# The last batch of an attention and expert kernel in another order: second group's scores in halves beside the first group's exponentials, batch 6's routing later

## The reference, cut to what matters

```
q = layernorm(x); k = v = ctx                 # (8, 256, 512)
qh, kh, vh = each.reshape(8 * 8, 32, 512)     # 8 heads of 32 rows
sm = softmax(einsum('bdm,bdn->bmn', qh, kh) / sqrt(32))
x = x + tanh(g) * einsum('bmn,bcn->bcm', sm, vh).reshape(8, 256, 512)
...
n = layernorm(x).reshape(2048, 512)
shared = (silu(n @ w_up_g) * (n @ w_up_y)) @ w_down
top 6 of sigmoid(n @ w_gate); position = running count per expert, over all tokens in order
routed = sum over 6 experts of weight * (silu(g) * v) @ w_down[e]
x = x + tanh(g) * (shared + routed)
```

## Time and profile before

| | |
|---|---|
| median of 3 runs | 1052.45 us (1051.8 to 1053.76) |
| the profiled execution's own time | 1051.3 us |
| its span, first to last instruction | 1049.5 us |
| TensorE busy | 990.5 us, 94% of the span |
| VectorE, ScalarE, POOL busy | 603.0, 335.0, 465.1 us |
| mean granted TensorE clock | 0.992 of full |
| main loop's last stages, batch 7's attention to the last scatter | some 637 to 720 us of the span |

### The profile page before, as it was taken

The page is one execution under the profiler, slowest core; times in us unless marked ns, Lnnn a source line. Parts: engine busy times, 40 slices in busy tenths (PEclk is TensorE's granted clock), DMA queues, the critical chain, the costliest instruction groups (busy, mean ns, idle before and its releaser), DMA issues.

```text
span 1049.5 us, 15353 instructions
## 1 busy us (share of the span) xinstructions
PE 990.5 (94%) x5629; PEld 603.6 (58%) x5630; DVE 603.0 (57%) x1249; ACT 335.0 (32%) x491; POOL 465.1 (44%) x457
## 2 busy tenths in 40 slices
PE   7999989999999999999999998895999999999886
PEld 6986545564564564464465452344777777776432
DVE  3334554765765855746756747543655556553566
ACT  3411024124133233323333231442444434443221
POOL 2000025526557467477467544352355555556000
PEclk9999999999999999999999999898999999999999
DMA  8793279697680590680610409356899999965998
GB/s 321 284 385 127 103 256 332 222 357 293 232 327 28 209 336 1 234 311 1 238 68 32 152 32 363 153 206 265 303 373 387 371 370 368 371 255 208 380 417 322
DMA packets 93622, 262.23 MB, mean 250 GB/s; under 512 B 10454, under 2 KB 10582, under 8 KB 92784
## 3 DMA queue, kind: packets, MB, share of 16 engines
q1 hardware_dynamic: 43760, 146.18, 38.0%
q10 hardware_dynamic: 31872, 63.97, 16.3%
q0 software_dynamic: 17920, 51.15, 12.4%
HBM read 129.91 MB, written 139.72 MB: 257 GB/s over the span
## 4 chain that ended last, share of the span: by engine, by line
PE 68%; DVE 8%; POOL 7%; DMA 7%; issue 6%; ACT 2%; SPq 0%; POOLq 0%; ACTq 0%; DVEq 0%
PE banks L1273 17%; PE banks L1892 11%; PE banks L1283 10%; DMA e_eo<-y_d 6%; PE banks L1881 6%; PE banks L1901 6%; POOL t_psum L773 5%; PE banks L1391 5%; PE banks L1453 5%; DVE t_nmx L1064 2%; PE banks L1471 2%; ACT t_probs L864 2%; DVE t_nmx L1073 1%; PE banks L1265 1%; PE banks L1456 1%
## 5 line engine op out<-in xcount | busy, mean ns | idle before, releaser
L1715 POOL DMA_INDIRECT y_d<-e_eo,e_ids x128 | 124.5, 973 | 126.3 <-DVE e_eo L1812 93.6
L1064 DVE TENSOR_REDUCE t_nmx<-banks 128x4 f32<-128x2048 f32 x56 | 128.1, 2287 | 58.3 <-PE banks L1391 58.3
L773 POOL TENSOR_TENSOR t_psum<-t_psum,t_probs 128x512 f32<-128x512 f32 x104 | 128.7, 1268 | 61.9 <-ACT t_probs L864 61.0
L864 ACT ACTIVATE t_probs<-banks 128x2048 f32<-128x2048 f32 x56 | 105.2, 1878 | 139.7 <-PE banks L1456 115.8
L785 POOL DMA_INDIRECT xs_d<-r_norm,r_xaddr x96 | 95.9, 998 | 49.2 <-issue 24.9
L1453 PE MATMUL banks<-b_qry,b_key 32*128 32x512 f32 x512 | 73.9, 647 | 7.9 <-ACT t_probs L864 5.7
L743 POOL TENSOR_TENSOR f_rstd<-f_veps,mhalf 128x2 f32<-128x2 f32 x24 | 16.8, 699 | 144.2 <-DVE f_veps L962 144.2
L1881 PEld LDWEIGHTS banks<-ident,e_xg 128*128 128x128 f32 x512 | 56.9, 143 | 34.3 <-issue 34.1
L1881 PE MATMUL banks<-ident,e_xg 128*128 128x128 f32 x512 | 63.9, 280 | 12.5 <-DMA e_xg<-xs_d 12.5
L773 POOL TENSOR_TENSOR t_psum<-t_probs,t_probs 128x512 f32<-128x512 f32 x52 | 66.5, 1316 | 12.4 <-ACT t_probs L864 6.3
L1391 PE MATMUL banks<-b_key,b_qry 32*128 32x512 f32 x448 | 63.9, 639 | 3.7 <-DVE t_nmx L1064 2.0
(11 more groups left out here) (227 smaller groups left out, 1646.7 us busy)
## 6 DMA issues: line engine op xcount, KB each, us to landing
xs_d<-zero ACTq DMA_DIRECT2D x32, 1056.0 KB, 7.1
e_xg<-xs_d SPq DMA_DIRECT2D x32, 1056.0 KB
y_d<-zero ACTq DMA_DIRECT2D x24, 1024.0 KB, 7.5
e_xg<-y_d SPq DMA_DIRECT2D x16, 768.0 KB, 14.8
e_eo<-y_d SPq DMA_DIRECT2D x16, 768.0 KB, 14.4
wo<-in_wud SPq DMA_DIRECT2D x6, 768.0 KB, 11.9
wupT<-in_wud SPq DMA_DIRECT2D x6, 768.0 KB, 11.7
a_x<-in_x SPq DMA_DIRECT2D x8, 512.0 KB, 4.7
```

The costliest lines, as they stand in the source:

```text
L773: ins = g_.tensor_tensor(psum0[:, q, :], first[:, q, :], probs[s % NP][:, q, :], ALU.add)
L864: A(probs[s % NP][:, :, :], quad[:, :, :], ACT.Exp, scale=SCALE1).then_inc(W["exp_ok"], 1)
L1064: V.tensor_reduce(nmx[g][:, m, :], quad[:, :, :], axis=AX.X, op=ALU.max, negate=True).then_inc(W["mx_ok"], 1)
L1715: g_.indirect_dma_start(out=y_d, out_offset=bass.IndirectOffsetOnAxis(ap=ids[:, HC * p + n:HC * p + n + 1], axis=0), in_=eo[u][:, n, :], i ...
```

## The change

It changes the tail of `ENDING` and what depends on it.

- The pieces of batch 7: before S0, S1 (halved), S2, S3 (halved), S4, S5, S6 (halved), S7, all ahead of the first Q. After: S0, S1 (halved), S2, S3 for the first group; then its P and M; and all four tiles of the second group halved, eight pieces in the pair, one after each Q and each V of the first group.
- Batch 6's turns, gates, choice and scatters (`R.turnA/6` to `R.x3/6`), which stood from `L.S6b` to `L.Q5`, come behind the second group's maxima, among Q4 to Q7 and behind V7. The order of batch 7's first half changes with it: `L.gates0` stands ahead of `L.Q7`, and `L.rows0a` behind `L.stats1`.
- The first shared product comes ahead of Q0; `L.up2` comes behind the second half's choice.
- SP loads three pairs of expert weights at first, and three more, with the early part of `e_acc`, behind `b_cT`.
- Banks and waits follow: `RELEASES`, `CHOSEN`, `L.S4a` waits for the copies of the two banks of the pair; the wait for batch 6's turns ahead of `L.V0` is gone; batch 6's second rows are kept at `L.K1`.

```
@@ ENDING
-F.down0/7 T.sum0c/6 T.Q5/6 F.down1/7 T.Q6/6 T.V3/6 T.Z0/6 T.Q7/6 F.stats3/7 R.x3/4 F.norm3/7 T.A0/6 L.V4/6 L.S0/7 L.S1a/7 L.V5/6 T.add0/6 R.x0/5
-L.S1b/7 L.S2/7 L.V6/6 L.V7/6 T.cT/7 T.A1/6 L.up0a/7 T.add1/6 R.x1/5 L.S3a/7 L.S4/7 L.S3b/7 L.up0b/7 L.P0/7 R.x2/5 R.stats/6 L.S5/7 L.S6a/7 L.M0/7 L.up0c/7 L.up0d/7
-R.norm/6 L.S7/7 L.S6b/7 R.turnA/6 R.turnB/6 R.x3/5 R.acc/5 R.acc/6 L.P1/7 L.Q0/7 R.gates/6 R.keep/6 L.Q1/7 L.V0/7 R.top/6 L.Q2/7 L.M1/7 R.pos/6 L.V1/7 L.Q3/7
-R.slots/6 R.x0/6 R.weigh/6 L.V2/7 R.x1/6 R.x2/6 L.Q4/7 L.V3/7 L.A0/7 L.add0/7 L.stats0/7 R.x3/6 L.Q5/7 L.V4/7 L.norm0/7 L.Q6/7 L.V5/7 L.turn0/7 L.Q7/7 L.gates0/7 L.top0/7
-L.V6/7 L.pos0/7 L.slots0/7 L.rows0a/7 L.V7/7 L.up1/7 L.A1/7 L.up2/7 L.add1/7 L.stats1/7 L.rows0b/7 L.norm1/7 L.turn1/7 L.gates1/7 L.top1/7 L.pos1/7 L.slots1/7 L.rows1/7
-L.weigh0/7 L.weigh1/7 L.up3/7 F.next/7
+F.down0/7 T.sum0c/6 T.Q5/6 F.down1/7 T.Q6/6 T.V3/6 T.Z0/6 T.Q7/6 F.stats3/7 R.x3/4 F.norm3/7 T.A0/6 L.V4/6 L.S0/7 L.S1a/7 T.add0/6 R.x0/5 L.V5/6 L.S2/7 L.S1b/7
+L.V6/6 R.x1/5 L.S3/7 L.V7/6 T.cT/7 L.more/7 L.up0a/7 L.up0b/7 L.P0/7 L.M0/7 L.K1/6 L.up0c/7 L.up0d/7 L.Q0/7 T.A1/6 L.S4a/7 R.x2/5 T.add1/6
+L.Q1/7 L.S4b/7 R.stats/6 L.V0/7 L.S5a/7 R.x3/5 L.Q2/7 L.S5b/7 L.V1/7 L.S6a/7 R.norm/6 L.Q3/7 L.S6b/7 L.V2/7 L.S7a/7 L.V3/7 L.S7b/7 L.P1/7 L.M1/7
+R.turnA/6 R.turnB/6 L.Q4/7 L.A0/7 R.gates/6 R.acc/5 R.acc/6 R.keep/6 R.top/6 L.Q5/7 R.pos/6 L.V4/7 R.slots/6 R.x0/6 L.add0/7 L.stats0/7 R.x1/6 L.norm0/7
+L.Q6/7 L.V5/7 L.turn0/7 R.weigh/6 L.gates0/7 L.Q7/7 L.top0/7 L.V6/7 L.pos0/7 R.x2/6 L.slots0/7 L.V7/7 L.up1/7 L.A1/7 L.add1/7 L.stats1/7 R.x3/6
+L.rows0a/7 L.rows0b/7 L.norm1/7 L.turn1/7 L.gates1/7 L.top1/7 L.pos1/7 L.slots1/7 L.rows1/7 L.weigh0/7 L.weigh1/7 L.up2/7 L.up3/7 F.next/7
@@ PIECES
-    ("L.S0", 0, 0, False), ("L.S1a", 1, 0, True), ("L.S1b", 1, 1, True), ("L.S2", 2, 0, False), ("L.S3a", 3, 0, True), ("L.S4", 4, 0, False),
-    ("L.S3b", 3, 1, True), ("L.S5", 5, 0, False), ("L.S6a", 6, 0, True), ("L.S7", 7, 0, False), ("L.S6b", 6, 1, True)))}
-CHOSEN = {("L.V4", 6): 2, ("L.up0a", 7): 3, ("L.M0", 7): 2, ("R.turnA", 6): 3, ("R.turnB", 6): 2}
+    ("L.S0", 0, 0, False), ("L.S1a", 1, 0, True), ("L.S2", 2, 0, False), ("L.S1b", 1, 1, True), ("L.S3", 3, 0, False),
+    *((f"L.S{n}{'ab'[half]}", n, half, True) for n in range(KC, 2 * KC) for half in range(2))))}
+CHOSEN = {("L.V4", 6): 2, ("L.up0a", 7): 1, ("L.M0", 7): 0, ("L.V0", 7): 2}
@@ SP
-            for p in range(len(wu)):
+            for p in range(first, end):
                 load_pair(sp, io, both, w_in, p)
...
+        def more_ahead(b):
+            pairs_ahead(3, 6)
+            for u in range(2):
+                sp.wait_ge(W[f"accst{u}"], 16 * 2)
+            early_acc(0, 4)
@@ ACT
-                  "L.M0": rows_of(0), "L.M1": rows_of(1), "L.V3": keep(0), "L.V7": keep(1)}
+                  "L.M0": rows_of(0), "L.M1": rows_of(1), "L.V3": keep(0), "L.K1": keep(1),
+                  "L.V7": lambda b: keep(1)(b) if b == LB else None}
@@ DVE
-                dve.wait_ge(W["mx_ok"], 8 * b + (KC * (g + 1) if b < LB else (7, 11)[g]))
+                dve.wait_ge(W["mx_ok"], 8 * b + (KC * (g + 1) if b < LB else (5, 13)[g]))
@@ PE
+                if name == "L.S4a":
+                    pe.wait_ge(W["mrow_ok"], 2 * b + 1)
+                    pe.wait_ge(W["raw_ok"], 1)
...
-                if (s, b) == (0, LB):
-                    pe.wait_ge(W["x4T_ok"], 2 * b - 1)
...
-                    pe.wait_ge(W["kept_ok"], 2 * b)
+                    pe.wait_ge(W["mx_ok"], 8 * b + PIECES["L.S1b"][0] + 1)
```

More of the change, by code:

```diff
@@ L507, in occupants @@
             lent = True
-        elif name == "L.S6b":
+        elif name == "L.S7b":
             holder[0:2] = [(name, b)] * 2
@@ L694, in first_pairs, with pairs_ahead @@
                 sp.wait_ge(W[n], 2 * NB)
+            pairs_ahead(0, 3)
+        def pairs_ahead(first, end):
             wu, wd, both = pair_weights(v)
-            for p in range(len(wu)):
+            for p in range(first, end):
                 load_pair(sp, io, both, w_in, p)
@@ L704, in loads_ahead @@
                 first_pairs()
-                for u in range(2):
-                    sp.wait_ge(W[f"accst{u}"], 16 * 2)
-                early_acc(0, 4)
+        def more_ahead(b):
[3 more added lines that the diff above has]
+            early_acc(0, 4)
         def r_acc(b):
@@ L721, in shared_rows @@
                 sp.dma_start(nrT[k][:, :, :], nrT_d[c, :, :].rearrange("p (k s) -> p k s", k=KC)).then_inc(W["nr_in"], 16)
-        steps({"F.keys": f_keys, "F.down1": loads_ahead, "T.cT": t_values, "F.next": f_next, "R.acc": r_acc, "R.keep": r_keep, "L.load": shared_rows})
+        steps({"F.keys": f_keys, "F.down1": loads_ahead, "L.more": more_ahead, "T.cT": t_values, "F.next": f_next, "R.acc": r_acc, "R.keep": r_keep, "L.load": shared_rows})
         sp.wait_ge(W["pv_mm"], 8 * NB)
```

## The result

The changed kernel takes 1063.27 us (median of 4 runs, 1062.13 to 1066.84), the kernel before beside it 1052.22 (4 runs, 1051.8 to 1053.76): ratio 1.0113, interval 1.0088 to 1.0137. It is slower by 11, where the forecast was slower by 4.6 and the range ended at 1061.5. The profiled execution has 1062.13, a span of 1060.4 and a mean granted clock of 0.985 (before: 1051.3, 1049.5, 0.992).

A forecast was written before the change was run, and what follows sets the result against it. Bound: the last batch's chain of waits to POOL's last scatter, then experts bound by TensorE. Terms -12.5 + 9.3 (to Q4) + 3.5 (to V7) + 4.3 (scatters) = +4.6 us, giving 1057.1; range 1054.0 to 1061.5.

The forecast's parts named there:

- First group: Batch 7's first maxima and split: fewer pieces ahead of Q0, which starts at 652.2 instead of 664.71, 12.5 us earlier.
- second group: Eight two-head pieces beside Q0 to Q3 take TensorE's time; of the 12.5 us gained only 3.2 is left.
- Q4: Fifth shifted-score step of batch 7: predicted to start at 678.2 instead of 681.4 us.
- pieces cheap: Two rivals on two-head pieces: costing TensorE nothing, 1049.6 us (chance 0.07), or half a four-head piece, 1054.0 us (0.10).
- the 3.2 that I counted: Gain left at Q4 after the second group's pieces: start at 678.2 instead of 681.4 us.
- Batch 6 behind the maxima: Batch 6's turns, gates, choice and scatters among Q4 to Q7 turn 3.2 us gained at Q4 into 0.3 lost at V7.
- the last scatters: On POOL behind the second reciprocal root: 15 scatters of 1.28 us end at 723.0 instead of 718.4, loss 4.6.
- Weights later: Three of six expert weight pairs and 2 MB of e_acc loaded behind b_cT: no effect, lying under the attention.
- Clock: Granted clock taken as 1.00 after the change: 3.2 us of low clock from 664.7 counted as saved, 0 taken as remaining.
- the two gaps behind it: TensorE idle for 2.9 us at 673.6 ahead of Q4, and 2.7 at 689 to 692 ahead of Q7.
- a low clock stays: Rival: a TensorE gap brings a low-clock stretch costing 3.2 us, 1060.3; two such, 1063; chance 0.30.
- a clock below 1.00 between 652 and 710: Sign that would show the forecast wrong: TensorE's granted clock under full in that stretch, in us, of the changed kernel.

The follow-up runs named there:

- bpool: Kernel before with only POOL's new order: batch 6's last three and batch 7's first four scatters behind the second reciprocal root; 1055.5 us, ratio 1.0028.
- fill: Changed kernel with two needless float32 matmuls in each of TensorE's two gaps, ahead of M1 and ahead of batch 7's first turn; 1057.86 us, ratio 1.0063.
- again: Changed kernel run once more, unaltered; 1063.97 us, ratio 1.0102 to the kernel before.
- x3: Changed kernel with batch 6's last three scatters moved ahead of the second reciprocal root on POOL; 1058.42 us, ratio 1.0056.
- q7v: Changed kernel with Q7 and V6 ahead of batch 7's first turn and gates, its count behind V7; 1062.21 us, ratio 1.0088.
- x3fill: Changed kernel with both gaps filled, batch 6's last three scatters ahead of the second root, and twelve needless matmuls ahead of the experts; 1055.49 us, ratio 1.0034.
- x3f2: Changed kernel with both gaps filled and batch 6's last three scatters ahead of the second root, no products ahead of the experts; 1055.37 us, ratio 1.0035.
- allfill: Changed kernel with both gaps filled, three scatters ahead of the second root, first root ahead of batch 6's scatters, Q7 and V6 earlier; 1056.22 us, ratio 1.0053.
- bfill: Kernel before with twelve needless matmuls while TensorE waits for the experts' first rows; 1051.07 us, ratio 0.9999.
- bgates: Kernel before with only the gates of batch 7's first half moved ahead of Q7; 1054.17 us, ratio 1.0017.

## Why the forecast was wrong

**First group, second group, Q4: right, the last to the hundredth by luck.** Forecast 16.6 and 42.6 after V4, measured 16.31 and 42.62. Between them two errors cancel: from Q0 to the last piece's end I had 21.4 and it took 22.2, since a two-head piece ahead of a V holds TensorE 1.06 (672.64 to 673.70) and not the 0.92 that I took from one row; and the wait behind was 2.48 and not 2.9. Two heads alone do hold TensorE like four, which leaves the two "pieces cheap" rivals out. What is gained at Q4 is less than it seemed: bpool, with the old order at full clock, has Q4 42.99 after V4, so the change brings 0.4, and the other 2.8 of the 3.2 that I counted was the low clock of 666.

**Batch 6 behind the maxima, and the last scatters: right.** Fill shows the forecast's walk at full clock: Q7 at 693.17 (693.3), the end of V7 at 698.41 (698.5), POOL's run from 703.81 (703.8), the end of the last scatter at 722.02 + 0.97 = 722.99 (723.0). That it is right to the tenth is luck: fill's V4 starts 0.45 earlier than the 635.60 that I walked from, so counted from V4 the walk is short by 0.3 to 0.5. Set against the kernel before as it was profiled, fill loses 94.67 - 89.73 = 4.94, forecast 4.6. Its median of 1057.86 is 0.8 from the 1057.1.

**Weights later: nil, as taken.** Nothing in the chain between V4 and the experts waits for them, in either kernel, and b_cT now lands in 3.9 (8.6 before).

**Clock: the step that failed.** It was "I take 0, since after the change TensorE is nearly always busy from 652 to 673". The reason was right for that stretch (7.75 busy of the 8 us from 658, clock 1.00) and beside the point: what mattered were the two gaps behind it, of 2.9 and 2.7 by my own sum, 2.48 and 2.21 measured. In all four profiles with these gaps open (after, again, x3, q7v) the clock fell behind one of them, between 676 and 704; in all four with products in them (fill, x3fill, x3f2, allfill) it fell nowhere between V4 and 704. Four against four is hardly chance, and the mean clocks of 20 and 22 executions (under fill) say the same. The term should have been 3.07, with the rival "a low clock stays" as the likely case and not at 0.30. I had named a clock below 1.00 between 652 and 710 as a sign of being wrong, and it came. I had counted the 3.2 of the kernel before (2.94 by the profiles) as saved and nothing as paid; in truth a stretch was exchanged for another of about the same price.

The Trainium skill (TensorE: Matmul & The Clock Gate, part 1) says that the array drops to half rate after an idle window; I wrote that by it nothing would drop ahead of the experts. The runs agree with its direction, since filling gaps of 2.48 and 2.21 us kept the clock up; they don't agree with what I drew from it, that gaps of this size are safe.

**The rest, 2.61, is no work of the change.** V4 starts at 638.21 in place of 635.60: less 0.3 that the changed kernel was ahead by at 142 us, plus 2.9 for the stretch there. This stretch came in nine of the twelve profiles, of both kernels, and in the three without it (before, fill, q7v) V4 starts at 635.15 to 635.60, otherwise at 637.44 to 641.02. The profiled execution of the kernel before happened to have none.

Summed, from the profiles: 7.88 for the order, less 2.94 (89.73 - 86.79) that the kernel before paid at 666, plus 3.07 at 694, plus 2.61 ahead of V4 is 10.62, which is what 735.95 - 725.33 gives. All terms are differences of the same few starts, so the sum has to close; that the clock's term is a price of its own is shown by x3 and x3f2 (3.09, and 3.05 in the medians).

**What the profile before hid.** Of the four profiles of the old order up to batch 7's first turn, only the one that I forecast from has the fall at 666 (bpool, bfill and bgates haven't), and only it lacks the stretch at 142. The two nearly cancel in its time, so it looked typical, but my walk from V4 counted 3.2 as saved that most executions of the kernel before don't seem to pay. Taking the other three as typical, which is an estimate from four profiles, the changed kernel should take 1052.2 + 7.88 + 3.07 = 1063.2; measured are 1063.27 and 1063.97. So the miss of 6.2 has two halves of about 3, both of the clock: a stretch credited that is mostly not there, and one taken at nothing that is. The range, up to 1061.5, had room for one of them. Why the fall at 666 stays away in three of four isn't settled.

## What to carry to other kernels

A gap that an edit opens in TensorE's work (here 2.2 and 2.5 us), just ahead of a stretch that TensorE bounds, can cost more than its own length: price it as the gap plus a low-clock stretch (here 3.1), and look at whether useful work can be laid into it. When a trace holds a low-clock stretch, take it out of both sides before an order is compared, or the one is credited with the other's luck. And where a queue issues at a steady pace (here 1.28 apiece), count what stands behind its last dependence, since each issue moved behind it moves the end one for one as long as the queue has no other wait.

## What was not expected of the hardware

- Four needless products, 3.96 us of TensorE work in all (two times 1.98), left the path 3.07 shorter, since they kept the granted clock at 1.00.
- The same program had its low-clock stretch at 694 to 702 in one execution and at 682 to 694 in another, each behind a gap (2.21, 2.48), and in the unchanged code at 142 or 146, behind a gap of 1.97, in nine of twelve profiles and in three not at all. Why a given gap brings a fall in one execution and not in the next stays open. A filled gap at 142 was not tried.
- Keeping the clock up for the experts' start gained nothing (bfill, ratio 0.9999): the first 48 transposes took 7.08 with waits for gathered rows between them, and 7.00 at the low clock.
